# Gathered rows transposed by VectorE blocks and SBUF transfers in place of TensorE, in a recommendation kernel

## What is computed

```python
e = jnp.stack([tbl_0[ids[:, 0]], ..., tbl_26[ids[:, 26]]], axis=1)
interactions = jnp.einsum('bnd,bmd->bnm', e, e)
z = interactions[:, i, j]                      # triu, k=1
h = jnp.concatenate([z, dense_ctx], axis=1)
h = jnp.maximum(h @ W_top1 + b_top1, 0.0)      # 367 -> 512
h = jnp.maximum(h @ W_top2 + b_top2, 0.0)      # 512 -> 256
y = h @ W_top3                                 # 256 -> 1
```

## Time and profile before

| | |
|---|---|
| median of 3 runs | 347.62 us (347.22 to 347.96) |
| span of the profiled execution | 346.3 us, 1.3 below that median (its own time is not listed apart) |
| PE busy | 331.1 us, 96% |
| DVE busy | 219.4 us, 63% |
| ACT busy | 184.7 us, 53% |
| POOL busy | 242.9 us, 70% |

### The profile page before, as it was taken

How to read it: one execution, slowest core, us unless ns; L and a number is a source line. 1 busy time by engine, 2 the same in 40 slices (tenths; PEclk the granted TensorE clock), 3 DMA queues, 4 the chain that set the end, 5 groups by cost and what they waited for, 6 DMA issues and landing times.

```text
span 346.3 us, 8212 instructions
## 1 busy us (share of the span) xinstructions
PE 331.1 (96%) x3478; PEld 282.8 (82%) x3478; DVE 219.4 (63%) x160; ACT 184.7 (53%) x315; POOL 242.9 (70%) x263
## 2 busy tenths in 40 slices
PE   2899999999999999999999999999999999998995
PEld 1667878887898888887898889887888889997894
DVE  5899997599427971499626991399724990360021
ACT  4898975533646354633646355633447346554521
POOL 6777777777777777777777777777777777777200
PEclk9999999999999999999999999999999999999999
DMA  6975795655237772768229772677327552572440
GB/s 169 222 178 168 225 252 142 156 157 135 67 55 157 146 158 55 107 173 178 83 55 157 146 160 55 89 197 177 83 57 134 131 112 57 85 168 72 85 81 8
DMA packets 53981, 44.06 MB, mean 127 GB/s; under 512 B 39810, under 2 KB 43983, under 8 KB 53945
## 3 DMA queue, kind: packets, MB, share of 16 engines
q1 hardware_dynamic: 43993, 26.52, 35.1%
q0 software_dynamic: 8192, 16.79, 21.3%
q10 hardware_dynamic: 1760, 0.22, 0.4%
HBM read 36.43 MB, written 7.09 MB: 126 GB/s over the span
## 4 chain that ended last, share of the span: by engine, by line
PE 86%; DMA 6%; SPq 3%; ACT 2%; issue 1%; DVE 1%; DVEq 0%
PE emb_ps L572 21%; PE emb_ps L574 20%; PE gram_ps L600 16%; PE mlp_ps L617 11%; PE mlp_ps L626 7%; PE emb_ps L583 7%; DMA h<-tbl_rows 3%; DMA products<-gram 1%; DMA gram<-tbl_rows 1%; PE emb_ps L644 1%; SPq L376 1%; DMA z<-products 1%; SPq L369 1%; PE mlp_ps L671 1%; PE mlp_ps L655 1%
## 5 line engine op out<-in xcount | busy, mean ns | idle before, releaser
L543 POOL DMA_INDIRECT rows<-tbl_rows,idx x256 | 242.0, 945 | 78.9 <-issue 74.4
L747 DVE TENSOR_TENSOR onehot<-ids_b,row_id 125x2048 fp32r<-125x2048 int32 x72 | 158.9, 2279 | 33.3 <-PE emb_ps L574 33.3
L572 PE MATMUL emb_ps<-onehot,table_hi 125*128 125x512 f32 (+1 forms) x400 | 147.6, 378 | 5.6 <-DVE table_lo L768 4.0
L574 PE MATMUL emb_ps<-onehot,table_lo 125*128 125x512 f32 (+1 forms) x400 | 143.0, 367 | 0.0
L572 PEld LDWEIGHTS emb_ps<-onehot,table_hi 125*128 125x128 f32 x400 | 76.0, 190 | 21.5 <-DVE table_lo L768 4.8
L574 PEld LDWEIGHTS emb_ps<-onehot,table_lo 125*128 125x128 f32 x400 | 76.1, 190 | 10.7
L600 PEld LDWEIGHTS gram_ps<-emb 128*54 128x54 f32 x2048 | 53.6, 130 | 5.6 <-issue 3.5
L600 PE MATMUL gram_ps<-emb 128*54 128x54 f32 x2048 | 55.8, 214 | 1.7 <-ACT emb L852 0.8
L851 ACT COPY held<-emb_ps 128x256 f32<-128x256 f32 x38 | 14.1, 371 | 75.9 <-PE emb_ps L574 75.8
L784 DVE TENSOR_TENSOR mlp_ps<-mlp_ps,rows 128x256 f32<-128x256 f32 x14 | 6.1, 433 | 76.5 <-PE mlp_ps L626 76.5
L882 ACT COPY gram<-gram_ps 118x432 f32<-118x432 f32 x64 | 33.2, 519 | 39.5 <-PE gram_ps L600 39.2
(11 more groups left out here) (49 smaller groups left out, 102.6 us busy)
## 6 DMA issues: line engine op xcount, KB each, us to landing
ids_b<-ids_onehot SPq DMA_DIRECT2D x33, 256.0 KB, 5.5
products<-gram SPq DMA_DIRECT2D x28, 216.0 KB
gram<-tbl_rows SPq DMA_DIRECT2D x9, 480.0 KB
rows<-tbl_rows,idx POOLq DMA_INDIRECT x256, 2.9
z<-products SPq DMA_DIRECT2D x14, 126.0 KB
h<-tbl_rows SPq DMA_DIRECT2D x2, 480.0 KB
z<-products SPq DMA_DIRECT2D x7, 112.0 KB
w_sb<-w SPq DMA_DIRECT2D x1, 768.0 KB, 5.8
```

Of the source, the lines that this page charges most:

```text
L543: pool.indirect_dma_start(out=rows[:, t, f, :], out_offset=None, in_=gathered_tables[f], in_offset=bass.IndirectOffsetOnAxis(ap=idx[:, p, ...
L572: nc.tensor.matmul(ps[:, 0:width], table_hi[0:ROWS, k, j, :], columns[:, c, :], start=j == 0, stop=False)
L574: last = nc.tensor.matmul(ps[:, 0:width], table_lo[0:ROWS, k, j, :], columns[:, c, :], start=False, stop=j == ROWS_PER - 1)
L747: nc.vector.tensor_tensor(onehot[0:ROWS, seq % ONEHOT_RING, 0:own * width].rearrange("p (j b) -> p j b", b=width), *operands, ALU.is_equal ...
```

## The change

For p > 0, six of the eight banks of a pair (all of tile 0, and the first half of tile 1) are no longer transposed by TensorE. A half tile is two banks, 8 features. VectorE transposes it in 32 x 32 blocks into `flips` (`flip_half`), SP moves the 16 blocks of partitions to their places in `moved` with 16 transfers of 32 partitions x 1 KB (`move_half`), and ACT copies `moved` into `emb` (`take_half`). Both buffers hold one half tile. There are 21 halves. The second half of tile 1 is still turned by TensorE, now behind the first tile's interaction products, and layer 2 stands ahead of the second tile's, in the last pair too. `rows` becomes a ring of five banks, and POOL waits for the reader of the bank five before instead of for `keep_back`'s places. The ids have four slots instead of five, and dense one place instead of two.

```diff
-IDS_SLOTS = 5
+IDS_SLOTS = 4
...
+ROW_BANKS = 5
+HALF_BANKS = 2
...
+def is_flipped(p, t, n):
+    return p > 0 and (t == 0 or n < HALF_BANKS)
...
+PIECES_BEFORE_FLIP = [0] + [8] * (PAIRS - 2) + [6]
+HALF_AFTER = 4
...
-        rows = sb("rows", [P, TILES, NG, DIM])
+        rows = sb("rows", [P, ROW_BANKS, TURNS_A_BANK, DIM])
+        flips = sb("flips", [P, BLOCKS, HALF_BANKS, TURNS_A_BANK, BLOCK])
+        moved = sb("moved", [P, BLOCKS, HALF_BANKS * TURNS_A_BANK, BLOCK])
...
+            def move_half(p, t, h):
+                number = HALF_NUMBER[(p, t, h)]
+                sp.wait_ge(flipped, FLIPPED_BY[(p, t, (h + 1) * HALF_BANKS - 1)])
+                if number > 0:
+                    sp.wait_ge(half_placed, number)
+                for q in range(BLOCKS):
+                    for b in range(BLOCKS):
+                        sp.dma_start(
+                            moved[b * BLOCK:(b + 1) * BLOCK, q, :, :].rearrange("p f j -> p (f j)"),
+                            flips[q * BLOCK:(q + 1) * BLOCK, b, :, :, :].rearrange("p g f j -> p (g f j)")
+                        ).then_inc(half_moved, 16)
...
+            move_half(1, 0, 0)
+            for p in range(1, PAIRS):
+                ids, ahead = lookups_of(p)[IDS_SLOTS:], lookups_of(p + 1)[:IDS_SLOTS] if p < LAST else []
+                for i in ids[0:2]:
+                    load_ids(i)
+                store_products(p - 1)
+                move_half(p, 0, 1)
+                load_z(p - 1)
+                load_dense(p)
+                for i in ids[2:]:
+                    load_ids(i)
+                for i in ahead[0:2]:
+                    load_ids(i)
+                move_half(p, 1, 0)
+                for i in ahead[2:]:
+                    load_ids(i)
+                if p < LAST:
+                    move_half(p + 1, 0, 0)
...
+            def free_row_bank(p, t, n):
+                number = bank_number(p, t, n) - ROW_BANKS
+                if number >= 0:
+                    earlier = ALL_BANKS[number]
+                    if is_flipped(*earlier):
+                        pool.wait_ge(flipped, FLIPPED_BY[earlier])
+                    else:
+                        pool.wait_ge(turned, TURNED_BY[earlier])
...
                         layer1(p - 1, m)
-                        turn(p, 1, m)
-                        if p == LAST and m == M1 // 2 - 1:
-                            gram_products(p, 0)
-                if p < LAST:
-                    gram_products(p, 0)
-                if 0 < p < LAST:
+                gram_products(p, 0)
+                if p > 0:
+                    for n in range(HALF_BANKS, TURN_BANKS):
+                        turn(p, 1, n)
                     layer2(p - 1)
                 gram_products(p, 1)
-            layer2(LAST - 1)
...
+            def flip_half(p, t, h):
+                number = HALF_NUMBER[(p, t, h)]
+                if number > 0:
+                    dve.wait_ge(half_moved, number * HALF_MOVED)
+                for g in range(HALF_BANKS):
+                    n = h * HALF_BANKS + g
+                    _, size = bank_features(p, n)
+                    dve.wait_ge(gathered[t][n], rows_gathered(p, n))
+                    nc.vector.transpose(flips[:, :, g, 0:size, :].rearrange("p b f j -> p f b j"),
+                                        row_bank(p, t, n).rearrange("p f (b i) -> p f b i", b=BLOCKS)
+                                        ).then_inc(flipped, 1)
...
+                for at, (i, part) in enumerate(pieces[ONEHOT_RING:], ONEHOT_RING):
+                    if at == ONEHOT_RING + 1:
+                        flip_half(p, 0, 1)
+                    elif at == PIECES_BEFORE_FLIP[p]:
+                        flip_half(p, 1, 0)
                     make_onehot(i, part)
+                if PIECES_BEFORE_FLIP[p] >= len(pieces):
+                    flip_half(p, 1, 0)
...
+            def take_half(p, t, h):
+                number = HALF_NUMBER[(p, t, h)]
+                act.wait_ge(half_moved, (number + 1) * HALF_MOVED)
+                first, _ = bank_features(p, h * HALF_BANKS)
+                last, size = bank_features(p, (h + 1) * HALF_BANKS - 1)
+                size += last - first
+                nc.scalar.copy(emb[:, t, :, first:first + size].rearrange("d (q j) f -> d q j f", j=BLOCK),
+                               moved[:, :, 0:size, :].rearrange("d q f j -> d q j f")).then_inc(half_placed, 1)
...
                         take_layer1(chunk, m)
-                        take_turned(p, 1, m)
-                        if p == LAST and m == M1 // 2 - 1:
-                            take_gram(p, 0)
+                    take_half(p, 1, 0)
                 if p == 0:
                     act.wait_ge(table_split, NO * GRAM_BANKS)
+                take_gram(p, 0)
                 if p < LAST:
-                    take_gram(p, 0)
                     place_dense(p)
+                if p > 0:
+                    for n in range(HALF_BANKS, TURN_BANKS):
+                        take_turned(p, 1, n)
```

More of the change, by code:

```diff
@@ L71, with bank_features, bank_number @@
 TURN_BANKS = -(-NG // TURNS_A_BANK)
+ROW_BANKS = 5
+HALF_BANKS = 2
+BLOCK = 32
+BLOCKS = P // BLOCK
+def bank_features(p, n):
+    end = min((n + 1) * TURNS_A_BANK, NG)
+    return n * TURNS_A_BANK, end - n * TURNS_A_BANK
+def is_flipped(p, t, n):
+    return p > 0 and (t == 0 or n < HALF_BANKS)
+def bank_number(p, t, n):
+    return (p * TILES + t) * TURN_BANKS + n
+ALL_BANKS = [(p, t, n) for p in range(PAIRS) for t in range(TILES) for n in range(TURN_BANKS)]
+TURNED = [bank for bank in ALL_BANKS if not is_flipped(*bank)]
+FLIPPED = [bank for bank in ALL_BANKS if is_flipped(*bank)]
+FLIPPED_HALVES = [(p, t, n // HALF_BANKS) for p, t, n in FLIPPED if n % HALF_BANKS == 0]
+TURNED_BY = {bank: n + 1 for n, bank in enumerate(TURNED)}
+FLIPPED_BY = {bank: n + 1 for n, bank in enumerate(FLIPPED)}
+PIECES_BEFORE_FLIP = [0] + [8] * (PAIRS - 2) + [6]
+HALF_AFTER = 4
+HALF_NUMBER = {half: n for n, half in enumerate(FLIPPED_HALVES)}
 def list_lookups():
@@ L102, in turns_ahead @@
 def turns_ahead(p, at):
-    banks = [(t, n) for t in range(TILES if p == 0 else 1) for n in range(TURN_BANKS)]
+    banks = [(t, n) for t in range(TILES if p == 0 else 0) for n in range(TURN_BANKS)]
     n = at - (len(cycle_lookups(p)) - len(banks))
@@ L117, in list_banks @@
         if p > 0:
-            out += [("turn", p * TILES + 1, n) for n in range(TURN_BANKS)]
+            out += [("turn", p * TILES + 1, n) for n in range(HALF_BANKS, TURN_BANKS)]
     return out
@@ L264, in build @@
         weights_loaded = sem("weights_loaded")
-        dense_loaded = [sem(f"dense_loaded{i}") for i in range(2)]
+        dense_loaded = sem("dense_loaded")
         dense_placed = sem("dense_placed")
@@ L326, in tile_end, with halves_by @@
         def tile_end(p, t):
-            last = BANK_INDEX[("turn", p * TILES + t, TURN_BANKS - 1)]
+            turns = [BANK_INDEX[("turn", p * TILES + t, n)] for n in range(TURN_BANKS) if (p, t, n) in TURNED_BY]
             looks = [BANK_INDEX[("look", i)] for i, lookup in enumerate(LOOKUP_LIST) if lookup[0] == p]
-            return max([last] + looks) + 1
+            return max(turns + looks) + 1
+        def halves_by(p, t):
+            return sum(half[:2] <= (p, t) for half in FLIPPED_HALVES)
         def store_position(engine, t, q):
@@ L543, in _ @@
                             pool.indirect_dma_start(
[L544 removed]
+                                out=rows[:, bank_number(p, t, n) % ROW_BANKS, f - first, :], out_offset=None, in_=gathered_tables[f],
                                 in_offset=bass.IndirectOffsetOnAxis(ap=idx[:, p, col:col + 1], axis=0),
@@ L579, in turn @@
                 ps = free_emb_bank(("turn", p * TILES + t, n))
-                first, size = turn_bank(n)
-                pe.wait_ge(gathered[t][n], (p + 1) * 16 * size)
-                for f in range(size):
-                    last = nc.tensor.transpose(ps[:, f * P:(f + 1) * P], rows[:, t, first + f, :], ident[:])
+                gathered_rows = row_bank(p, t, n)
+                pe.wait_ge(gathered[t][n], rows_gathered(p, n))
+                for f in range(bank_features(p, n)[1]):
+                    last = nc.tensor.transpose(ps[:, f * P:(f + 1) * P], gathered_rows[:, f, :], ident[:])
                 last.then_inc(turned, 1)
```

111 lines of the change are left out of this document (44 added, 67 removed).

## The result

The changed kernel takes 443.15 us (median of 4 runs, 440.69 to 444.9) against 347.51 (median of 4, 347.22 to 347.96; the table of before has three of them): a ratio of 1.2743, interval 1.269 to 1.2796. The sign is as predicted, and so is the place: VectorE waits for moves. Its size is not: +35 us were forecast, +96 came, outside the range. The profiled execution took 444.69 us, its span is 442.9.

The account below looks back on a forecast made before the run. TensorE and POOL's gathers were taken as bounds within 1%. Three 10-piece cycles at +2.3, three 12-piece at +6.7 and +7.9 in the last gave 34.9 on 346.3, so 381.2; with 1.3 above the span, 382 us, range 357 to 402.

Parts of the forecast that it names:

- What bounds it: Whole kernel before: TensorE busy 96% of the span, POOL's gathers 1.250 us a step, two bounds within 1%.
- the sign: Whole kernel: the change makes it slower, chance 0.93.
- the rivals of no change: Whole kernel: everything hidden and gathers decide, 350.5 us, chance 0.07, of it 0.02 that no change can be told.
- the rival "faster": POOL's gathers: the 0.30 us between them comes from being held back, pitch falls towards 0.945, 332 us; chance 0.05.
- What VectorE gets: Lookups: 42 block transposes at 0.62 us (0.55 to 0.87), cycles +0.9 us with 10 pieces, +1.3 with 12.
- the other estimate in the prediction, 1.24: VectorE's block transposes: the skill's 311 ns taken four times, 1.24 us each and 2.5 us more a cycle.
- What ACT gets: ACT's 21 copies of half tiles: 2.06 us each (lower end 1.42), TensorE waiting 1.4 us a cycle (lower end 0.8).
- What SP gets: SP's 336 issues: 0.40 us each, 6.4 a half; VectorE waits 4.0 us in 12-piece cycles, none in 10-piece.
- no wait, no slack: 10-piece cycles: the move is issued by 12.0 us and lands at 14.4, just when VectorE needs its buffer.
- The last cycle: Last pair to the end: z load and moves come late, end at about 54.5 us, +7.9 (+5 to +12).
- The gathers: POOL with five banks: held back some 5 us at the tightest, costing nothing while cycles are the slower side.
- The heavy rival (400 to 415): SP's queue: issues slow down behind the products' many small packets, 400 to 415 us; chance 0.08.

Follow-up runs that it names:

- without moves: Changed kernel with no transfers of the halves: VectorE writes two buffers in turn, ACT copies from them, partition exchange left out; 366.27 us, ratio 1.0488.
- four moves: Changed kernel with only the 4 diagonal transfers of the 16 of each half, the other blocks staying zero; 366.45 us, ratio 1.0493.
- small transposes: Changed kernel without any transfers of the halves, each block transpose also cut from 512 elements to 32; 358.21 us, ratio 1.0249.
- four issues of 128 KB: Changed kernel with each half moved in 4 transfers of 128 partitions x 1 KB, partition exchange left out; 369.82 us, ratio 1.0609.

## Why the prediction was wrong in size and right in kind

**What bounds it, the sign, and the rivals of no change.** Right. That the removed transposes are worth nothing while POOL gathers at 1.25 us a step was argued from the earlier trace rows and is shown by the run that leaves them out (0.9997). The 0.30 us stand before 243 of the changed kernel's 256 gathers too (74.1 us), where `keep_back` is gone, so the rival "faster" has no ground.

**What VectorE gets.** Right: 0.65 to 0.69 us against 0.62 (the other estimate in the prediction, 1.24, is nearly twice that), and cycles of 44.3 and 39.9 once moves are cheap, to 0.3 us the sum's own.

**What ACT gets.** Right in the copy (2.02 against 2.06), and nearly in the stall: 1.13 us a cycle (7.9 / 7, without moves) against 1.4. That the cycles come out to 0.1 us is in part luck: this miss and that of the transposes (4 x 0.03) have opposite signs.

**What SP gets: the step that failed.** "Issue times in the trace are 0.319 us (table rows), 0.407 (ids) and 0.535 (dense, 16 rows of 1 KB). I take 0.40, 6.4 us a half, and keep 0.32 to 0.58 (5.1 to 9.3)." Measured: 0.59 for one issue, 0.635 from one to the next, 10.1 to 12.0 us a half. The whole range was too low, although a row of before had the warning: the loads of `z` take 2.52 us for 3 issues and the stores 4.75 for 4, 0.84 and 1.19 each. I bounded the unknown price by the cheapest issues and left out the dearest. Those ends would have given 5.1 to 19 us a half.

The Trainium skill (DMA: Bandwidth & Descriptors, Anatomy of one DMA, which describes GpSimd's path) puts sequencer dispatch at about 50 ns and says that many descriptors can be emitted before the incremental cost shows. Carried over to SP's queue, of which that section does not speak, it would make a half an estimated 0.8 us of issuing (16 x 50 ns). The rows of SP's and ACT's queues have medians of 0.591 to 0.616 us for a move, with 32 or 128 partitions alike; the measurement decides.

**What hangs on it.** Put the measured 10.2 us for a half into the prediction's own sum. In a 12-piece cycle the stores end at 9.6 us, the move at 19.8 and lands at 22.2: VectorE would wait 7.8 instead of 4.0. In a 10-piece cycle the move would be issued from 5.6 to 15.8 and land at 18.2: 3.8 instead of none. The last cycle has two such halves one behind the other, 7.6. That is an estimated 30 of the missing 61 us.

The second part of the miss: I costed each half alone and never added up SP's cycle. In pair 3 SP comes to the stores at 4.85 us (172.85), as predicted, but they take 7.01 us instead of 4.75, and the move 11.20 instead of 10.2; so VectorE waits 10.46. The kernel before had the warning in the same cycle, in a row that I did not take:

```profile
141.96 6.29 SPq L376 DMA_DIRECT2D products<-gram  x4
```

Three halves, stores, loads and ids fill 48 of 55.6 us, and the third half can't be issued before ACT has copied the second (29.6 us of SP's waits, 6.4 here). So SP enters the next cycle late: the stores of pair 4 begin 2.1 us in instead of 0.6, the move is issued by 17.5 and VectorE waits 4.38 us where I had "no wait, no slack". Ids come late too (10.3 us of VectorE's waits). How the other 31 us divide between this and the clock was not measured.

**The clock.** Not in the prediction at all. The view by stretches of the changed kernel (stretch, us, busy time and count of PE, PEld, DVE, ACT, POOL, granted clock, DMA share, GB/s):

```profile
236.00:244.00 8.00, 4.12 (x16) 2.74 (x16) 3.62 (x4) 3.34 (x5) 5.90 (x7) 1.00 0.41 112
244.00:258.00 14.00, 12.02 (x56) 9.85 (x58) 11.69 (x7) 3.01 (x7) 9.44 (x10) 0.76 0.61 152
...
385.00:415.00 30.00, 16.04 (x168) 14.01 (x168) 2.97 (x3) 8.71 (x12) 4.54 (x5) 0.72 0.27 74
```

TensorE waits for VectorE in the first stretch and comes back at a lower clock in the second, a mixture of its two levels, 1.2 and 2.4 GHz. The same 3310 matmuls are busy for 341.5 us in the changed kernel and 325.6 with four moves: 15.9 us more of matmul time go with the lower clock (0.903 over the span against 0.995), on top of the waits. The first matmul after a wait takes longer as well (0.50 us at 167.94, then 0.39), and the two were not told apart. Not all of it lies on the path.

**The last cycle.** Predicted at 54.5 us (its terms, 37.7 + 8.4 + 8.7, add up to 54.8), measured at 69.9 from TensorE's first lookup at 373.0. Point by point from that start, predicted and measured: layer 1 begins at 17.4 and 26.5, the second half lands at 25.3 and 37.5, first products end at 29.7 and 42.8, second ones at 37.7 and 50.7. The order of events is the predicted one. SP still issues the half before until 377.6 us, 4.6 into the cycle, and the two halves behind it take 10.6 and 10.9 us instead of 6.4; layer 1 itself runs in part at the lower clock (0.67 granted from 399.5 to 408.0 us):

```profile
399.52 8.21 PE L672 MATMUL mlp_ps<-z,w_sb 126*128 126x256 f32 x24 [10.56 <-DMA z<-products]
```

8.21 us where it takes 5.2 otherwise.

**The gathers.** "The banks then land before VectorE asks" holds only while cycles are slow, as the prediction's own condition said. With four moves VectorE already waits 6.1 us for rows, with small transposes 22.7. POOL was held back for up to 13.5 us at a time in the changed kernel, which cost nothing there: no engine waits for gathered rows in its view of waits.

**The heavy rival (400 to 415).** Nearer in time than my range, wrong in mechanism: it had the issues slow down behind the products' small packets. Fifteen of the sixteen behind the stores in pair 3 take 0.59 us; only the first is longer (1.42 us at 179.96 in the chain). What did grow was the stores themselves, 7.01 us.

**The account.** Of 95.6 us, 76.7 are the twelve extra issues a half, with all that SP delays by them and the clock that the pauses cost. Of the 18 that stay (366.45 against 348.59), the transposes are worth 8.1, ACT's place for the copy 3.3 and the tail's order 3.3 when each is taken away alone. The second is hardly clear of the spread of its runs, and the third was measured in the kernel before. They need not add up, since VectorE's waits for gathered rows take part of each back; what the last 3 us are was not measured.

Still open: a move in fewer issues that exchanges the blocks' partitions without a way through DRAM, and second buffers for `flips` and `moved` were not tried. No version beats the kernel before. The run without the 42 groups shows that taking them off TensorE is worth nothing while the gathers and the tail behind them stay as they are.

## What to carry to other kernels

Count the issues of a queue over a whole cycle, as for an engine, before the bytes: here 48 issues of 0.635 us are 30 us of a cycle that took 40, while 8 times the bytes made an issue no longer than 0.60. Bound an unknown issue time by the dearest rows of the same queue, and take the pitch of a run (time of the run by its count), not the time of one. Ahead of taking work from a full engine, leave that work out in an experiment: if the time stays, another bound lies behind it, and what replaces the work has nothing to gain there.

## What was not expected of the hardware

A transfer within SBUF held the issuing engine for 0.59 to 0.62 us (medians), for 16, 32 or 128 KB and on SP's queue as on ACT's. In the trace of before, table loads from DRAM cost 0.319, ids 0.407, and stores and loads of products about twice that or more. Why they differ was not tested.

A store of 512 KB from SBUF to DRAM landed 5.1 us after its issue.

Where TensorE had paused, its granted clock was lower: 0.76 from 244 to 258 us, around a pause of 5.83 that ended at 245.98, and 0.72 from 385 to 415, around one of 10.56. A pause of 2.6 us was enough once: from 381.5 to 384.5, behind it, the clock was 0.50 of full speed, the lower level. The span's mean fell from 1.000 to 0.903. Where TensorE waited at most 2.4 us for a one-hot (four issues of 128 KB) the mean was 0.982.
